# Fifteen row normalisations moved from VectorE to GpSimd, behind the reciprocal root

## What is computed

```
x = x + attn(layernorm(x))                    # n = 0: 128 heads, latent attention
x = x + xattn(layernorm(x), ctx, positions)   # n = 1: 32 query heads, 8 key heads, rope
x = x + ffn(layernorm(x))                     # n = 2: a base product, 8 low-rank experts, the best 2 weighted

layernorm(x) = (x - mean(x)) / sqrt(var(x) + 1e-5)      # over the 512 features of each token
```

## Time and profile before

| what | value |
|---|---|
| time, median of 3 runs | 828.34 us (828.11 to 830.26) |
| profiled execution, own time | 826.78 us |
| its span | 824.5 us |
| TensorE matmuls busy | 793.0 us, 96% |
| VectorE busy | 628.6 us, 76% |
| ScalarE busy | 582.7 us, 71% |
| GpSimd busy | 590.9 us, 72% |
| granted TensorE clock, mean | 0.998 |

### The profile page before, as it was taken

One profiled execution on the slowest core, in us unless ns is written; L12 is line 12 of the kernel. 1 busy time (PEld: TensorE's weight loads), 2 busy tenths in 40 slices (PEclk: granted clock), 3 DMA queues, 4 the chain that ended last, 5 costly groups with the idle time before them and its releaser, 6 DMA issues.

```text
span 824.5 us, 17894 instructions
## 1 busy us (share of the span) xinstructions
PE 793.0 (96%) x5641; PEld 391.9 (48%) x5641; DVE 628.6 (76%) x1190; ACT 582.7 (71%) x1072; POOL 590.9 (72%) x535
## 2 busy tenths in 40 slices
PE   5999999999999999999999999999999899999987
PEld 3464444444444444444444444444444444555444
DVE  6766676676677788776788876778878888888766
ACT  8757777777777777777777777778765655666551
POOL 7967999999988888887888887878655634222111
PEclk9999999999999999999999999999999999999999
DMA  9344355533434333343333344352321000000001
GB/s 344 124 172 142 93 142 161 162 98 89 104 107 120 90 79 93 89 128 100 100 81 97 83 119 107 92 158 63 88 61 48 27 2 2 14 14 13 18 15 39
DMA packets 52176, 75.80 MB, mean 92 GB/s; under 512 B 10256, under 2 KB 34096, under 8 KB 51616
## 3 DMA queue, kind: packets, MB, share of 16 engines
q1 hardware_dynamic: 52128, 75.23, 32.8%
HBM read 38.69 MB, written 19.40 MB: 70 GB/s over the span
## 4 chain that ended last, share of the span: by engine, by line
PE 87%; DVE 4%; ACT 3%; issue 2%; SPq 2%; DMA 1%; POOL 0%; DVEq 0%; ACTq 0%
PE PS L1567 40%; PE PS L1639 7%; PE PS L1606 7%; PE PS L1640 7%; PE PS L1501 6%; PE PS L1654 5%; PE PS L1740 2%; PE PS L1832 2%; PE PS L1679 1%; PE PS L1798 1%; PE PS L1616 1%; PE PS L1688 1%; PE PS L1839 1%; PE PS L1817 1%; PE PS L1849 1%
## 5 line engine op out<-in xcount | busy, mean ns | idle before, releaser
L1567 PE MATMUL PS<-XTh,W 128*128 128x512 f16 x1024 | 346.0, 379 | 0.0
L656 POOL TENSOR_TENSOR Pl<-PR,Ph 128x512 f16<-128x512 f32 x254 | 285.8, 1156 | 28.4 <-ACT Ph L938 28.4
L931 ACT ACTIVATE PR<-PS 128x512 f32<-128x512 f32 x256 | 152.8, 597 | 131.7 <-PE PS L1640 124.9
L1125 DVE TENSOR_REDUCE mneg<-PS 128x4 f16<-128x512 f32 x256 | 171.6, 685 | 35.3 <-PE PS L1606 33.4
L1567 PE MATMUL PS<-XTl,W 128*128 128x512 f16 x512 | 193.6, 378 | 0.0
L1113 DVE SCALAR_TENSOR_TENSOR QS<-PS,QC 64x512 f16<-64x512 f32 x256 | 175.5, 685 | 20.8 <-ACT QC L848 16.7
L848 ACT ACTIVATE QC<-PS 64x512 f16<-64x512 f32 x256 | 150.7, 589 | 9.2 <-PE PS L1567 4.3
L1567 PEld LDWEIGHTS PS<-XTh,W 128*128 128x128 f16 x1024 | 96.6, 97 | 118.8 <-issue 25.9
L938 ACT ACTIVATE Ph<-PR 128x512 f16<-128x512 f32 x256 | 139.3, 617 | 0.0
L1606 PEld LDWEIGHTS PS<-KC,QC 112*128 112x128 f16 x1024 | 78.4, 97 | 63.5 <-issue 2.7
L1606 PE MATMUL PS<-KC,QC 112*128 112x128 f16 x1024 | 99.4, 219 | 0.9 <-ACT QC L848 0.8
(11 more groups left out here) (236 smaller groups left out, 1034.1 us busy)
## 6 DMA issues: line engine op xcount, KB each, us to landing
Wraw<-in_wqr SPq DMA_DIRECT2D x32, 512.0 KB, 4.8
QS<-QC SPq DMA_DIRECT2D x64, 256.0 KB, 3.2
head_outputs<-OS SPq DMA_DIRECT2D x256, 40.0 KB
q_content_parts<-stg SPq DMA_DIRECT2D x12, 256.0 KB, 2.9
k_content_parts<-stg SPq DMA_DIRECT2D x12, 256.0 KB, 3.1
QC<-q_content_parts SPq DMA_DIRECT2D x116, 24.0 KB
KC<-k_content_parts SPq DMA_DIRECT2D x29, 96.0 KB
xs<-in_x SPq DMA_DIRECT2D x8, 256.0 KB, 4.8
```

Source lines behind the costliest of these rows:

```text
L656: nc.gpsimd.tensor_tensor(Pl[:, 4 * j.s + b], PR[:, b], Ph[:, 4 * j.s + b], ALU.subtract).then_inc(s_pl, 1)
L931: nc.scalar.activation(PR[:, b, :], PS[:, bB[b % 2], :], ACT.Exp, scale=ATT_SCALE).then_inc(s_e, 1)
L1125: nc.vector.tensor_reduce(mneg[:, j.p, j.s, :, b], PS[:, bA[b % 2], :].rearrange("p (j k) -> p j k", j=GH), AX.X, ALU.max, negate=True).th ...
L1567: last = mm(PS[:, bQ[c], :], wt[:, j.w, k, c * P:(c + 1) * P], xt[:, k, sl], start=(i == 0), stop=(i == 3 * KT - 1))
```

## The change

GpSimd computes the rows itself, directly behind its root, for all tiles of n = 1 and n = 2 but the last. `norm_rows` is no longer called in the loop on VectorE; its one call behind the loop, for n = 2 and tile 7, stays. The waits move along: on GpSimd the rows wait for the root's own semaphore `n_sd[n]`, and from tile 2 on for the turn of tile v - 2 (`n_tp[n]`). The operation, its operands and its output buffer are the same. Fifteen instructions change their engine.

```diff
@@ -785,6 +785,12 @@
                 if 0 <= b < B:
                     pool.wait_ge(n_var[n], b + 1)
                     nc.gpsimd.tensor_tensor(rstd[:, n, b:b + 1], rstd[:, n, b:b + 1], power[:], ALU.pow).then_inc(n_sd[n], 1)
+                    if (n, b) != (2, B - 1):
+                        pool.wait_ge(n_sd[n], b + 1)
+                        if b >= 2:
+                            pool.wait_ge(n_tp[n], b - 1)
+                        nc.gpsimd.tensor_scalar(pn[n][:, b % 2], xs[:, b, :], mv[:, n, b, 0:1], rstd[:, n, b:b + 1],
+                                                ALU.subtract, ALU.mult).then_inc(n_xn[n], 1)
 
             done = [0]
 
@@ -1412,14 +1418,11 @@
                     x_max(2 * u + 5)
                 if u == -2:
                     norm_low(1, b + 2, bF[0])
-                if r == 2:
-                    norm_rows(1, b + 2)
                 if r == 3:
                     x2(b - 1, bF[1])
                 if 0 <= u - 1 < NU:
                     x_outputs(u - 1)
                 if r == 0:
-                    norm_rows(2, b - 2)
                     if 0 <= b + 1 < B:
                         v = b + 1
                         dve.wait_ge(s_xq, v + 1)
```

## The result

The changed kernel takes 831.22 us (median of 20 runs, 829.2 to 832.95), the kernel before, on the same chip, 827.09 us (20 runs, 825.85 to 830.26). The ratio is 1.0047, 95% interval 1.0039 to 1.0055: slower by 3.9 us (3.2 to 4.5); the medians themselves differ by 4.1. I had forecast +1.15 us, no telling difference. The time itself lies at the upper end of my range. The profiled execution of the changed kernel has a span of 831.2 us and a time of 832.95, the longest of its twenty; that of before has a span of 824.5 and lies 0.3 us under its median.

The account below looks back on a forecast made before the run. TensorE was taken to bound the last quarter. Terms 0.5 (late tiles) + 0.8 (keys' rope) - 0.45 (experts' first tile) + 0.3 (block 2) = +1.15 us on 828.34 gave 829.5 us, range 826.7 to 831.2.

Parts of the forecast that it names:

- my three signs of being wrong: Rows over 1.1 us, the rope instructions running through, or a new wait for a row in the steady blocks.
- The row's price: One normalised row on GpSimd was taken as 0.77 us, upper end 1.27, against VectorE's 0.557.
- my four places: Cross attention's first and second tiles, experts' tile 6, keys' rope; a 1.09 us row would add about 0.9 us in sum.
- Rival 3: Row costs 1.27 instead of 0.77 us, like the two-input sum: together +3.1, 831.5 us; chance 0.11.
- First and second tile: Cross attention's first two normalised tiles are ready later than TensorE could start them: +0.2 us each.
- my own formula: A GpSimd row is ready 0.1 us plus its own 0.77 after its root ends, 0.87 in all.
- Tile 6 of the experts: Row about 0.2 us late near 804 us, but only TensorE's weight load comes late: +0.1 us.
- The keys' rope: Rope of the keys' second half, 653 to 659 us: VectorE waits longer for GpSimd's delayed instructions, about +0.8 us.
- Experts' first tile: At 682 to 685 us VectorE loses a row ahead of the query's rope, TensorE idles less: -0.45 us.
- rival 2: Keys' rope gains instead of losing and the clock stays up at 685 us: 826.6, at most 825.8; chance 0.09.
- Block 2: Experts' block 2, 690 to 698 us: later GpSimd work holds VectorE's small comparisons, TensorE's query late by 0 to 0.6, taken +0.3.
- The rest: Bias sum 0.9 us earlier per block, new wait long fulfilled, no DMA moves, last tile stays on VectorE: no time added.

Follow-up runs that it names:

- the last version: Kernel before with (add, mult) rows on GpSimd except the cross attention's first three and experts' last two tiles, last weight split at unit 6: ratio 0.9984, 825.66 us.

## Where the prediction was right and where it was wrong

The time, 831.22 us, stands at the very end of the range that I gave, 826.7 to 831.2, and that is luck. I had started from three runs with a median of 828.34; twenty runs on the same chip give 827.09. The change itself is +3.9 us, where I had forecast +1.15 and my range allowed +2.9. Of my three signs of being wrong one came in full, rows of over 1.1 us, and one nearly, the rope instructions running through; no new wait appeared in the steady blocks. So the number was near and the cause was wrong.

**The row's price.** This is the step that failed: "I take 0.77, the same operation with one tensor read, and keep 1.27 as the upper end". L615 of the earlier trace rows is (mult, add), the new row (subtract, mult), which takes 2.08 us. Not only the value but the upper end was wrong, since I asked for the number of tensors read and not for the pair of operations; L615's source showed the difference. By the Trainium skill's factor of two (GPSIMD Engine Reference, section Performance versus the Vector engine) I had 1.09. The measured ratio is 3.7 for this pair and 1.4 for (add, mult), so that rule holds for neither here. Its own example is a sum of two inputs, and for that this trace comes near it: 1.268 us for 128x512 against 0.691 on VectorE, 1.8 times. What I made of it was also too little: 0.32 us more at each of my four places is 1.3 us, not 0.9.

With the price right, the number would have stood: the kernel with rows of 0.767 us came out at 1.0014, +1.2 us (0.2 to 2.2), where I had +1.15. That too is partly luck. Counted from the start of its first root its turns show 0.22 at the first tile, 0.04 at the second, +0.48 at the keys, -0.45 for the relief, -0.66 for the clock and +0.83 in block 2, in all 0.5 us. The terms do not come out as I had them. Rival 3, a row as slow as the two-input sum, is nearest to what happened, at a price far beyond the 1.27 that I had given it, and I gave it 0.11.

**First and second tile**: +0.2 each predicted. The mechanism is right; with 2.08 instead of 0.77 my own formula gives 1.5 each, measured 1.54 and 1.12. With 0.767 the waits are 0.16 and 0.27. **Tile 6 of the experts**, +0.1: about right, even with the slow row. TensorE had come later too, and only the load of its weights waited for the row, 0.32 us; the turn began 0.09 behind the matmuls ahead of it.

**The keys' rope**: +0.8 predicted, -0.92 measured in the changed kernel, because the slow row pushed the weight scaling so far back (660.18 us) that VectorE's four instructions had almost only the short instructions of kst beside them (L1272 took 1.15 us and L1275 1.04, against 0.76 and 0.69 undisturbed), and TensorE's 0.86 us wait went. In the kernel with the price that I had assumed the mechanism worked as told, L1272 at 2.68 us and +0.48. The lower end of the forecast's own range, 828.8, follows from no bound that I named: this place at +0.06 and block 2 at 0 give 828.4. The Trainium skill's rule (SBUF — State Buffer, section Who interferes with whom), that the one which starts first holds the port for its whole length, has these rows on its side.

**Experts' first tile**: -0.45 predicted, 1.76 to 1.31 us of idle time measured in every kernel with that row gone from VectorE. The clock then stayed up in the changed kernel (0.65 us more), which I had as rival 2.

**Block 2**: +0.3 predicted, range 0 to 0.6. Mis-sized: the small comparisons were held for about as long as the GpSimd instruction lasted. It was 0.83 at a row of 0.767. At 2.08 it was 1.8, and 3.50 where the clock fell behind it.

**The rest**: right for the time. The steady blocks showed the same waits for KQ. Two things were not as I had said: VectorE was to be busy 8 us less and was busy 0.3 us less, and its sum of the query was held after all.

## What to carry to other kernels

Price a moved instruction by a row with the same operations on the same engine, not by its shape; where there is none, the bounds must be wide. On GpSimd write a normalisation as add and mult with a negated mean: 0.77 us instead of 2.08 here. Ask what a longer queue pushes into the other engine's work: here three small comparisons behind a weight split cost 1.8 us, beside some 3 us for the late tiles, and moving that split three units ahead won them back. And leave the rows on the fast engine wherever the reader already stands waiting.

## What the runs showed of the hardware

- GpSimd's tensor_scalar on 128x512 float32 took 0.78 to 0.83 us for (mult, add) and (add, mult) with per-row scalars, 2.10 with a subtraction in either place, 1.58 and 1.56 for one operation alone; with constants 0.63 and 1.94.
- A VectorE comparison of 64 elements with two SBUF inputs, 0.21 us alone, took up to 1.20 us beside GpSimd's two-input instructions. VectorE's row, which reads one tensor and two per-row scalars, took 1.46 instead of 0.55 beside one.
- The granted clock behind an idle time of 1.31 us at the experts' first tile stayed at 1.00 in the profiles of nine kernels and fell to 0.50 in one (the last version, 686 to 688 us), with the same 1.31. Behind 1.76 or 1.77 us it fell each time, in four. In block 2 it stayed behind 1.65 and 1.66 us in two kernels and fell behind 1.66 and 1.89 in two. The same kernel differs between executions as well: 7 of 33 runs of the kernel before have a mean clock of 1.000, where its profile, with one fall, has 0.998. What decides it stays open.
- VectorE's busy time fell by 0.3 us when instructions of 8.4 us left it: time in which an instruction is held counts as busy.
- Between 800 and 812 us the clock fell for a few microseconds in 11 of 14 profiled executions, whatever the kernel, and cost about 1.5 us. A difference of that size between two single profiles tells nothing of a change.
